# Second norm on ScalarE, VectorE's turns in an order of their own, and five sends in two units

## What is computed

```python
xn = _layernorm(x, axis=-1)
x = x + gnn(xn, edge_index, edge_weight, W, b) + mix(xn)
xn2 = _layernorm(x, axis=-1)
gate_logits = xn2 @ Wg + bg + bias
topk_vals, topk_idx = jax.lax.top_k(gate_logits, 2)
topk_w = jax.nn.softmax(topk_vals, axis=-1)
h = relu(einsum('td,edh->teh', xn2, W1) + b1)
y = einsum('teh,ehd->ted', h, W2) + b2
out = x + einsum('ted,te->td', y, combine)   # combine: topk_w at topk_idx
```

## Time and profile before

| | |
|---|---|
| median of three runs | 3717.16 us (3711.85 to 3720.75) |
| the profiled execution | 3712.03 us |
| its span, first to last instruction | 3710.3 us |
| TensorE matmul busy in the span | 2723.5 us, 73% |
| VectorE | 2553.0 us, 69% |
| GpSimd | 2548.0 us, 69% |
| ScalarE | 628.5 us, 17% |
| mean granted clock of TensorE | 0.907 of full |

### The profile page before, as it was taken

How to read it: one execution, slowest core, us unless ns; L and a number is a source line. 1 busy time by engine, 2 the same in 40 slices (tenths; PEclk the granted TensorE clock), 3 DMA queues, 4 the chain that set the end, 5 groups by cost and what they waited for, 6 DMA issues and landing times. The chain is left out here.

```text
span 3710.3 us, 69265 instructions
## 1 busy us (share of the span) xinstructions
PE 2723.5 (73%) x16161; PEld 2235.5 (60%) x16165; DVE 2553.0 (69%) x6668; ACT 628.5 (17%) x1326; POOL 2548.0 (69%) x2390
## 2 busy tenths in 40 slices
PE   1447776577777777676676667667767999999998
PEld 1346666366566665555555555555533788888887
DVE  9999999455555555677777777777768566654444
ACT  8312222411111111000000000000013221112221
POOL 7347777677777777777777777777745477775444
PEclk9987777789999999888899898998877999999999
DMA  5545555634444444444444444444457455555443
GB/s 173 167 144 183 180 184 158 222 117 128 127 125 128 125 124 126 131 131 125 131 131 131 129 127 131 131 131 124 125 177 220 73 115 114 112 114 92 73 75 52
DMA packets 327621, 492.01 MB, mean 133 GB/s; under 512 B 60714, under 2 KB 247854, under 8 KB 327214
## 3 DMA queue, kind: packets, MB, share of 16 engines
q0 software_dynamic: 127584, 270.17, 28.9%
q1 hardware_dynamic: 161029, 176.37, 15.6%
q10 hardware_dynamic: 38601, 41.04, 3.5%
HBM read 376.35 MB, written 111.03 MB: 131 GB/s over the span
## 5 line engine op out<-in xcount | busy, mean ns | idle before, releaser
L770 POOL DMA_INDIRECT message<-h_table,records x1616 | 1549.9, 959 | 511.5 <-issue 498.4
L1278 PE MATMUL bank<-message,select 128*128 128x256 f32 x3232 | 924.5, 436 | 566.7 <-issue 296.6
L1278 PEld LDWEIGHTS bank<-message,select 128*128 128x128 f32 x3232 | 665.4, 215 | 781.7 <-issue 404.2
L1821 DVE TENSOR_SCALAR select<-iota_n,records 128x128 f32<-128x128 f32 x1660 | 594.3, 358 | 501.4 <-PE bank L1278 486.9
L1829 DVE TENSOR_TENSOR acc<-acc,bank 128x256 f32 x1660 | 683.4, 412 | 9.9 <-PE bank L1278 6.0
L823 POOL DMA_INDIRECT out<-acc,row_of x210 | 331.7, 1580 | 302.5 <-DVE acc L2356 152.5
L735 POOL DMA_INDIRECT lists<-placed,dest_i x300 | 348.5, 1162 | 201.2 <-ACT placed L957 106.9
L1514 PE MATMUL bank<-w,acc 128*128 x1680 | 387.1, 384 | 19.7 <-DVE acc L2340 19.7
L1501 PE MATMUL bank<-fx_t,acc 128*128 128x256 f32 x1680 | 380.1, 379 | 2.5 <-ACT fx_t L1096 2.5
L1514 PEld LDWEIGHTS bank<-w,acc 128*128 128x128 f32 x1680 | 315.6, 193 | 61.5 <-issue 21.5
L1501 PEld LDWEIGHTS bank<-fx_t,acc 128*128 128x128 f32 x1680 | 318.7, 190 | 46.0 <-ACT acc L1103 1.9
(11 more groups left out here) (356 smaller groups left out, 3579.2 us busy)
## 6 DMA issues: line engine op xcount, KB each, us to landing
fetched<-h_table SPq DMA_DIRECT2D x3200, 1.0 KB
fetched<-h_table ACTq DMA_DIRECT2D x2432, 1.0 KB
rows<-block_dram SPq DMA_DIRECT2D x75, 514.5 KB
acc<-x_sorted SPq DMA_DIRECT2D x105, 260.0 KB, 3.1
message<-h_table,records POOLq DMA_INDIRECT x1616
xt_in<-xt_dram SPq DMA_DIRECT2D x98, 256.0 KB
lists<-zeros_list SPq DMA_DIRECT2D x8, 1664.0 KB, 14.9
read_back<-lists SPq DMA_DIRECT2D x13, 1024.0 KB, 7.0
```

The lines of the kernel that those rows point to most:

```text
L770: pool.indirect_dma_start(out=message[:, k % SETS, j, :], out_offset=None, in_=h_table, in_offset=Offset(ap=records[:, k * SET + j, 0:1], ...
L1278: last = nc.tensor.matmul(ps, select[:, slot % 2, j, :], rows_of, start=True, stop=True)
L1821: return V.tensor_scalar(select[:, k % 2, j, :], iota_n[:, :], records[:, k * SET + j, 1:2].bitcast(F32), records[:, k * SET + j, 2:3].bit ...
```

## The change

ScalarE normalises the pairs, with the scale rstd and a bias mean_shift = -mean x rstd that VectorE makes once a turn (s_scaled), two pairs ahead of the slot. VectorE's gate_turn is gone: it works through whole turns of statistics (stats_turn) and whole stretches of routing in a written order. ScalarE takes the root of the next turn at the fourth slot of a turn, not the third; counts and exponents stand at slots 14 and 30, not 13 and 20. In the unit loop GpSimd sends three and two copies by turns, from unit 2 on, and the blanks from unit 62.

```diff
--- before.py
+++ after.py
@@ -131,13 +131,13 @@
     BLANK_UNIT = EXPERTS * REGION
     DUMP = (BLANK_UNIT + 1) * 2 * P
     UNIT_RING = 4
-    FIRST_PARTS = 2
+    FIRST_PARTS, COUNT_AT = 2, [14, 30]
     ROUTE_FIRST, ROUTE_PACE, STEPS_PER_SLOT = 5, 10, 4
     SENDS = 4 * TURN
-    SEND_AT = [None, None, 3] + [ROUTE_FIRST + ROUTE_PACE * (t - 3) + 7 for t in range(3, TURNS)]
-    BLANKS_AT = SEND_AT[TURNS - 1] + 10
+    SEND_AT = [None, None, 2] + [ROUTE_FIRST + ROUTE_PACE * (t - 3) + 7 for t in range(3, TURNS)]
+    BLANKS_AT = UNIT_FROM[TURNS - 1] - 15
     TABLE_AT = [None, None] + [SEND_AT[t] + 8 for t in range(2, TURNS - 1)] + [SEND_AT[TURNS - 1] + 13]
-    assert PAIRS == TURNS * TURN and UNITS <= P and KH == 4 and BLANKS_AT + 12 < UNIT_FROM[TURNS - 1]
+    assert PAIRS == TURNS * TURN and UNITS <= P and KH == 4 and BLANKS_AT + 11 < UNIT_FROM[TURNS - 1]
     assert all(TABLE_AT[t] < UNIT_FROM[t] and SEND_AT[t] + 14 <= UNIT_FROM[t] + 1 for t in range(2, TURNS))
     assert N % P == LAST and NB % TB == 0 and EXPERTS == 8
     assert KC * HID == KH * C and NB % 4 == 2 and KC == 2 and 4 * C == 1024 and HID == 512
@@ -320,6 +320,7 @@
         blank_pos = sb("blank_pos", [P, 2, EXPERTS], I32, route)
         fxn_t = sb("fxn_t", [P, 2, KC, 2 * P], F32, route)
         logit_t = sb("logit_t", [EXPERTS, 4, 2 * P], F32, route)
+        mean_shift = sb("mean_shift", [P, NB], F32, route)
         newton_turn = sb("newton_turn", [P, TB], F32, route)
         route.close()
 
@@ -431,6 +432,7 @@
         s_xtile_dram = sem("s_xtile_dram")
         s_xtile_row = sem("s_xtile_row")
         s_fxn = sem("s_fxn")
+        s_scaled = sem("s_scaled")
         s_sent = [sem(f"s_sent{i}") for i in range(2)]
         s_fx = [sem(f"s_fx{i}") for i in range(UNIT_RING)]
         s_fxt_psum = sem("s_fxt_psum")
@@ -835,7 +837,7 @@
             blanks = list(range(2 * EXPERTS))
             for u in range(UNITS):
                 if u >= SEND_AT[FIRST_PARTS]:
-                    for _ in range(3):
+                    for _ in range(3 - u % 2):
                         if waiting and u >= SEND_AT[waiting[0][0]]:
                             t, i = waiting.pop(0)
                             if i == 0:
@@ -1073,18 +1075,32 @@
 
                 act.wait_ge(s_route, t * 2 + 1)
                 act.activation(top_w[:, 1, :], small[:, 4, :], ACT.Exp).then_inc(s_route, 1)
+
+            def normalise(g):
+
+                if g % TURN == 0:
+                    turn = g // TURN
+                    act.wait_ge(s_scaled, turn + 1)
+                    act.wait_ge(s_kept[turn], 32 if turn == TURNS - 1 else 16)
+                for b in (2 * g, 2 * g + 1):
+                    last = act.activation(acc[:, b, 0:C], acc[:, b, 0:C], ACT.Identity, bias=mean_shift[:, b:b + 1], scale=rstd[:, b:b + 1])
+                last.then_inc(s_fxn, 1)
             root(0)
+            normalise(0)
+            normalise(1)
             for g in range(PAIRS):
+                if g + 2 < PAIRS:
+                    normalise(g + 2)
                 act.wait_ge(s_xt_psum, PAIRS + g + 1)
                 if g >= 2:
                     act.wait_ge(s_logit_psum, g - 1)
                 act.activation(fxn_t[:, g % 2, :, :].rearrange("p k n -> p (k n)"), bank[g % 2][:, :], ACT.Identity).then_inc(s_xt, 1)
                 if g:
                     copy_logits(g - 1)
-                if g % TURN == 2 and g // TURN + 1 < TURNS:
+                if g % TURN == 3 and g // TURN + 1 < TURNS:
                     root(g // TURN + 1)
-                if g % TURN == TURN - 1 and 0 < g // TURN <= FIRST_PARTS:
-                    softmax_exp(g // TURN - 1)
+                if g in COUNT_AT:
+                    softmax_exp(COUNT_AT.index(g))
             copy_logits(PAIRS - 1)
             softmax_exp(FIRST_PARTS)
 
@@ -1462,8 +1478,8 @@
                 last.then_inc(s_route_psum, 1)
             for g in range(PAIRS):
                 f_transpose(g)
-                if g % TURN == TURN - 1 and 0 < g // TURN <= FIRST_PARTS:
-                    count_tokens(g // TURN - 1)
+                if g in COUNT_AT:
+                    count_tokens(COUNT_AT.index(g))
                 if g:
                     gate(g - 1)
                 if g > 1:
@@ -1932,11 +1948,6 @@
                 steps.done(V.tensor_tensor(r, r, n, ALU.mult))
                 steps.settle()
 
-            def normalise(g):
-                for u in range(2):
-                    b = g * 2 + u
-                    last = V.tensor_scalar(acc[:, b, 0:C], acc[:, b, 0:C], row_mean[:, b, 0:1], rstd[:, b:b + 1], ALU.subtract, ALU.mult)
-                last.then_inc(s_fxn, 1)
             steps.done(V.memset(v_sb[:, :, :, P:P + 2], 1.0))
             steps.settle()
 
@@ -2016,6 +2027,8 @@
 
             def invert_turn(turn):
                 invert_std(turn + 2, turn * TB, TB, newton_turn[:, :])
+                blocks = slice(turn * TB, turn * TB + TB)
+                V.scalar_tensor_tensor(mean_shift[:, blocks], row_mean[:, blocks, 0], -1.0, rstd[:, blocks], ALU.mult, ALU.mult).then_inc(s_scaled, 1)
 
             def read_logits(turn):
                 dve.wait_ge(s_gate, turn * TURN + TURN)
@@ -2038,28 +2051,13 @@
                 for _ in range(count):
                     next(routes[t], None)
 
-            def gate_turn(turn):
-
-                dve.wait_ge(s_kept[turn], 32 if turn == TURNS - 1 else 16)
-                for j in range(TURN):
-                    normalise(turn * TURN + j)
-                    if turn and j == 3:
-                        read_logits(turn - 1)
-                    if turn < TURNS - 1 and j < 3:
-                        for b in range(j * 5, min(j * 5 + 5, TB)):
-                            block_stats(turn * TB + TB, b)
-                    if turn < TURNS - 1 and j == 2:
-                        gather_stats(turn * TB + TB)
-                    if turn in (1, 2) and 3 <= j < 6:
-                        choose(turn - 1, 9 if j < 5 else 100)
-                    elif turn in (2, 3) and j < 3:
-                        place(turn - 2, 14 if j < 2 else 100)
-                if turn < TURNS - 1:
-                    invert_turn(turn + 1)
-            for j in range(TB):
-                block_stats(0, j)
-            gather_stats(0)
-            invert_turn(0)
+            def stats_turn(turn):
+                for j in range(TB):
+                    block_stats(turn * TB, j)
+                gather_stats(turn * TB)
+                invert_turn(turn)
+            stats_turn(0)
+            stats_turn(1)
             dve.wait_ge(s_fin, 48)
             dve.wait_ge(s_const, 5)
             steps.done(V.tensor_copy(reached[:, :], region[:, 0, :]))
@@ -2294,10 +2292,26 @@
                 V.engine_nop().then_inc(s_blank_at, 1)
                 yield
             routes = [route_part(t) for t in range(TURNS)]
-            for turn in range(TURNS):
-                gate_turn(turn)
-            choose(FIRST_PARTS, 100)
-            read_logits(TURNS - 1)
+            PLACED = 12
+            stats_turn(2)
+            read_logits(0)
+            choose(0, 100)
+            place(0, PLACED)
+            read_logits(1)
+            stats_turn(3)
+            place(0, 100)
+            stats_turn(4)
+            read_logits(2)
+            choose(1, 100)
+            place(1, PLACED)
+            read_logits(3)
+            stats_turn(5)
+            read_logits(4)
+            stats_turn(6)
+            place(1, 100)
+            read_logits(5)
+            choose(2, 100)
+            read_logits(6)
 
             def route_beside(u):
```

## The result

The changed kernel takes 3679.72 us (median of five runs, 3677.93 to 3688.21) against 3711.85 for the kernel before beside it: a ratio of 0.9916, 95% interval 0.9898 to 0.9935, 32 us less. The profiled execution took 3679.72 us, with a span of 3678.0 and a mean granted clock of 0.912 (3710.3 and 0.907 before).

What follows compares the result with a forecast made beforehand. It took the norm stage as held by VectorE's normalise and the loop as TensorE-bound at 7.35 us a unit plus 28.9 us of GpSimd-made stalls. Gains 27 + 4 = 31 us: 3717.16 - 31 = 3686, range 3670 to 3707.

Steps and rivals of the forecast that it cites:

- rival (a): Norm stage: ScalarE and TensorE keep their clock, VectorE is ahead of the roots; first unit at 2875, total 3675; 9%.
- GpSimd makes them: Unit loop: GpSimd's 7.57 us a unit against TensorE's 7.35 makes it late and causes the 28.9 us of stalls.
- The sends, 27 us: Unit loop: three and two sends by turns cut GpSimd to 6.94 us a unit, gaining 27 us, ends 12 and 28.
- The jump of the lag at a list: Unit loop: a list write holds one landing back, so GpSimd's next add lags 4.7 us.
- worked off at 0.4 a unit in 12 units: Unit loop: GpSimd's lag behind a list shrinks 0.4 us a unit; 0.7 is left over at the next write.
- rival (b): Unit loop: lag adds up over lists, stalls at the third and fourth; 12 to 17 us gained, total near 3700; 17%.
- it just doesn't wait: Unit loop: VectorE needs an add's landing after 12.4 us and a held one takes 11.8, so no wait.
- Normalise on ScalarE: Norm stage: ScalarE takes the normalise, 1.08 us a pair, near 1.8 us a slot, equal to TensorE's 1.78.
- the upper end of 2.06 us: Norm stage: ScalarE's slot time if neighbours do not overlap, costing 10 us over 38 slots.
- VectorE's order: Norm stage: ScalarE's roots wait about 6, 9 and 3 us for statistics; first unit at 2886, 4 us gained.
- (c): Norm stage: clock stays low behind ScalarE's first wait, about 20 slots, 25 us; first unit at 2911, total 3711; 8%.
- (d): Norm stage into units: low clock from slot 18 to 48 and beyond; start at 2919, total 3726, slower; 6%.

Runs made afterwards that it cites:

- norm_only: The changed kernel with the old sends, three in every unit, and the old blanks: 3705.18 us, ratio 0.9977 to the kernel before.
- before128: The kernel before the change with only the lists written as 128 pieces of 12 bytes, not 384 of 4: 3680.25 us, ratio 0.9908.
- the seven executions: Profiled executions of the kernels with five sends in two units and small list pieces: stalls 8.2 to 16.9 us, 13.3 in the mean.
- sends_only: The kernel before, old norm stage kept, with five sends in two units and the later blanks: 3694.86 us, ratio 0.9949.
- list128: The changed kernel with lists written as 128 pieces of 12 bytes and read back by three short transfers: 3670.42 us, ratio 0.9883.
- order: The changed kernel with part 1's last routing and turn 6's statistics ahead of reading turn 4's logits: 3686.14 us, ratio 0.9929.

## Why the total was right and its terms were not, point by point

The time came out at 3680 where 3686 was forecast, within the range, between the forecast and rival (a)'s 3675. Of the 6 us between them 5 are the kernel before, which took 3711.85 beside the change and not the 3717.16 that the forecast starts from. The sum of 31 us was met by 32.3 in the trace, but that is luck, by two errors that cancel: the sends were taken at 27 and gave 20, the stage was taken at 4 and gave 12 in itself and 9.5 in the time.

**Stalls are the loop's loss, and lists strike there.** Right: the gaps stand at units 29, 39 and 54 of norm_only, one unit around each list. But the text put GpSimd's pace first ("GpSimd makes them"). before128 shows the shares: with the pace left at three sends and only the lists' pieces made larger, 22 of the 28.9 us go.

**The sends, 27 us.** The jump of the lag at a list, taken at 4.7 us, was right in the mean: 3.2, 5.7, 2.9, 6.5 and 5.7 us at the five lists of the changed kernel, 4.8 on average. The step that failed is "worked off at 0.4 a unit in 12 units". It nearly held behind the first list, where the lag fell from 4.0 to 1.0 us in nine units, 0.33 a unit. Behind the second it fell from 6.7 to 5.0, 0.19 a unit, and from unit 26 to 56 it stayed between 6 and 7.7 apart from the jumps, which took it to 13.4 and 12.1 us at the last two lists; these two stall TensorE (gaps of 9.72 and 12.33 us at units 39 and 54). The text took GpSimd's 6.94 us a unit from instructions alone. The measured pace, when it is late, is 7.66 us after three sends, not 7.57, and mostly 6.4 to 7.3 after two, not 6.30, since the add waits for the landing of the one before. Over stretches of six or seven units between lists the mean is 7.16 to 7.49 (the adds of the changed kernel at units 49 to 56 and 25 to 31), against TensorE's 7.35, so there 0.2 us a unit is spare at best; behind the first list (units 4 to 13) it was 7.02.

This is the mechanism of rival (b), the lag that adds up. (b) was to leave 12 to 17 us gained in the loop; the seven executions gained 12 to 21, and 15.6 in the mean (28.9 less 13.3), and sends_only's medians gave 19.9. The 28.9 are themselves one execution; norm_only, with the same sends, had 31.6. So in the loop (b) has the mechanism, and its size or somewhat better; the stage's 12 us kept the total from (b)'s 3700. The step "it just doesn't wait" (12.4 us against 11.8) fell with it: VectorE waited 47 times, 9.3 us at the longest.

**Normalise on ScalarE.** Right: 584 ns each, pairs of 1.08 us, and a slot of 1.765 us at full clock. ScalarE, busy for 16.78 of 18 us, had a little to spare, and the upper end of 2.06 us did not occur.

**VectorE's order.** Right as a mechanism: three waits of the root, of 4.3, 7.6 and 2.6 us for the 6, 9 and 3 foretold, at slots 17, 31 and 38; SyncE's list was the last of the three ends. The whole chain was too late: slot 3 at 2764.4 and not 2768.5, as the low level held for two slots only; the last list at 2860.6 and not 2869; the first unit at 2877.3 and not 2886. The clock's loss behind a wait was over after 5 to 6 us, for the 8 assumed.

**What the stage's 12 us are.** Of them some 5.5 were in none of the prediction's terms: the hole of the old stage beside its second list. I had read the old stage's excess over 49 full slots as VectorE's and the clock's alone; before128 moves it by 6.4 us with VectorE's work untouched. The changed kernel writes that list at 2860.59 and its slots run on at 1.76 to 1.77 us beside it. That the change escapes the hole by the list's new time, and not by anything else, fits norm_only, list128 and order, but isn't shown by an experiment of its own.

**Rivals.** (a), a better stage, is half true: with the roots' waits gone the first unit came 123.0 us behind the statistics, close to its 124.4, and still the time did not move, for GpSimd's sends and the loop took it. (c) and (d) did not occur: the half clock held for 6 us behind the first wait, and came back each time.

## What to carry to other kernels

Where one engine's lateness shows at regular places, look at what other transfer goes out there before making the engine's work lighter: here 384 pieces of four bytes once in nine to fifteen units cost the old loop 22 of its 28.9 us of stalls, and making them 128 was worth as much as the whole change (0.9908 alone, 0.9883 with it). Count an engine's pace between two issues that wait for each other's landing, not from its instructions' lengths. And when a loop's stalls hang on where two streams meet, take several executions before crediting a few microseconds to an edit ahead of it.

## What the runs showed of the hardware

- A write of 384 pieces of 4 bytes could be read back 8.7 to 11.9 us later (70 lists in ten executions), and 2.4 to 6.0 us with 128 pieces of 12 bytes (28 lists in four). An indirect add issued 1.3 us ahead of such a write landed so late that the next add started 13.39 us behind it; with the larger pieces, an add issued 0.5 us ahead, it was 8.09 us.
- In the changed kernel the queue of that write had no packet from 3144 to 3150.8 us, though the read that waits for the write went out only at 3150.84.
- Beside such a write in the norm stage ScalarE stood still for 2.8 to 5.3 us with no partner named (VectorE and TensorE too in some), in four kernels of four that wrote it between 2837 and 2842 us; the two that wrote it in large pieces at 2830 and 2836 had no such stop, nor had the changed kernel, which wrote it in small ones at 2860.59.
- Two indirect adds of 128x256 f32 land 6.1 us behind the first one's issue, though they occupy GpSimd for 3.5 us.
- TensorE was back at 2.4 GHz 5 to 6 us after it took up work again behind idle times of 5.70 and 9.06 us (2801.38 to about 2807, and 2838.76 to about 2844.5, in the changed kernel).
